# Layer norm normalised by ScalarE, and a rebuilt first batch, in a two-layer ternary feed-forward kernel on one core

## The reference, cut to what matters

```python
h = relu(einsum(x, w1[lang]) + b1[lang])            # 256 -> 64
v = x + einsum(h, w2[lang]) + b2[lang]              # 64 -> 256
normed = (v - mean(v)) * rsqrt(var(v) + 1e-5)
z = normed * gamma[lang] + beta[lang]
def bitlinear(x, W, b):
    w_scale = clip(mean(abs(W)), EPS)
    Wq = clip(round(W / w_scale), -1, 1) * w_scale
    x_scale = clip(max(abs(x), axis=-1), EPS)       # per token
    xq = clip(round(x * 127 / x_scale), -128, 127) * x_scale / 127
    return xq @ Wq.T + b
x = x + bitlinear(gelu(bitlinear(z, W1, b1)), W2, b2)   # 256 -> 1024 -> 256
```

## Time and profile before

| what | value |
|---|---|
| median of 3 runs | 342.05 us |
| the three runs | 339.6, 342.05, 342.3 us |
| the profiled execution | 338.81 us, of which the span from first to last instruction is 336.9 us |
| mean granted TensorE clock | 0.939 |
| layer 0 up to the first instruction of layer 1's dequantisation | 168.0 us |
| layer 1 from there | 168.9 us |

### The profile page before, as it was taken

The page is one execution under the profiler, slowest core; times in us unless marked ns, Lnnn a source line. Parts: engine busy times, 40 slices in busy tenths (PEclk is TensorE's granted clock), DMA queues, the critical chain, the costliest instruction groups (busy, mean ns, idle before and its releaser), DMA issues.

```text
span 336.9 us, 6456 instructions
## 1 busy us (share of the span) xinstructions
PE 270.9 (80%) x1640; PEld 177.6 (53%) x1640; DVE 287.9 (85%) x633; ACT 221.2 (66%) x341; POOL 264.8 (79%) x440
## 2 busy tenths in 40 slices
PE   0783849998799988899777799798989989766775
PEld 0322324563446455466544578576666757535652
DVE  0199599999999989887399899999999999999661
ACT  0641787776667777773256797877778687877560
POOL 2068898888988878862899999898989999899520
PEclk9955898999999999999799989999999999999786
DMA  7987306587879897477681044669677575554863
GB/s 223 298 220 270 110 2 154 135 219 186 192 184 198 184 258 168 115 149 163 175 255 58 2 82 123 173 156 178 142 166 183 102 177 142 90 142 109 180 149 94
DMA packets 97002, 53.10 MB, mean 158 GB/s; under 512 B 74165, under 2 KB 90301, under 8 KB 96966
## 3 DMA queue, kind: packets, MB, share of 16 engines
q1 hardware_dynamic: 95078, 51.43, 62.4%
q10 hardware_dynamic: 1888, 1.27, 1.3%
HBM read 27.51 MB, written 8.39 MB: 107 GB/s over the span
## 4 chain that ended last, share of the span: by engine, by line
issue 28%; POOL 20%; PE 17%; DVE 17%; DMA 8%; ACT 5%; SPq 4%; DVEq 1%; POOLq 0%; ACTq 0%
POOL mid L713 8%; DMA q1T<-r 6%; PE banks L1146 4%; POOL raw_all L720 3%; PE banks L1132 3%; PE banks L1091 3%; POOL xb L693 3%; PE banks L1263 2%; DVE amy L919 2%; DVE xb L913 2%; PE banks L1133 2%; DVE xb L937 2%; POOL dq L704 1%; DVE zg L849 1%; DVE am L950 1%
## 5 line engine op out<-in xcount | busy, mean ns | idle before, releaser
L720 POOL TENSOR_TENSOR raw_all<-raw_all,mid 128x1024 f32<-128x1024 f32 x32 | 64.0, 2014 | 0.2 <-DVE raw_all L944 0.2
L564 ACT ACTIVATE banks<-xb,taps 128x512 f32<-128x512 f32 x64 | 43.6, 689 | 22.5 <-DVE xb L937 22.5
L713 POOL TENSOR_SCALAR mid<-xb,taps,convb 128x512 f32<-128x512 f32 x64 | 49.7, 786 | 2.1 <-DVE xb L937 2.1
L944 DVE SCALAR_TENSOR_TENSOR raw_all<-xb,taps,banks 128x512 f32<-128x512 f32 x64 | 45.6, 735 | 0.0
L937 DVE TENSOR_TENSOR xb<-banks,dqb 128x512 f32<-128x512 f32 x64 | 42.6, 680 | 1.0 <-PE banks L1237 1.0
L1263 PE MATMUL banks<-tern,q1T 128*128 128x256 bf16 x256 | 36.2, 289 | 8.5 <-DVE o L971 5.3
L880 DVE TENSOR_REDUCE am<-g 128x1 f32<-128x1024 f32 x32 | 38.6, 1205 | 3.7 <-ACT g L510 3.7
L1237 PE MATMUL banks<-yT,tern 128*128 128x512 bf16 x128 | 35.0, 383 | 7.4 <-ACT yT L550 3.9
L1146 PE MATMUL banks<-tern,q1T 128*128 128x256 bf16 x256 | 34.1, 277 | 8.4 <-DMA q1T<-r 6.3
L950 DVE TENSOR_REDUCE am<-g 128x1 f32<-128x1024 f32 x32 | 38.7, 1208 | 1.7 <-ACT g L570 1.7
L666 POOL TENSOR_SCALAR r<-g,qs 128x1024 uint16<-128x1024 f32 x24 | 30.8, 1281 | 11.7 <-DVE qs L892 11.7
(11 more groups left out here) (108 smaller groups left out, 561.2 us busy)
## 6 DMA issues: line engine op xcount, KB each, us to landing
xr<-in_x SPq DMA_DIRECT2D x8, 512.0 KB, 4.2
x_after_layer<-x SPq DMA_DIRECT2D x16, 256.0 KB, 2.5
x<-x_after_layer SPq DMA_DIRECT2D x8, 512.0 KB, 3.6
xr<-x_after_layer SPq DMA_DIRECT2D x8, 512.0 KB, 3.8
out_y<-o SPq DMA_DIRECT2D x32, 128.0 KB, 2.0
xT<-in_xT SPq DMA_DIRECT2D x4, 512.0 KB, 4.1
x2T<-in_xT SPq DMA_DIRECT2D x4, 512.0 KB, 5.4
wl<-in_cwl SPq DMA_DIRECT2D x8, 256.0 KB, 3.3
```

The costliest lines, as they stand in the source:

```text
L564: act.activation(bank(BANK_U[g % 3]), apad[:, f, 2:S + 2], ACT.Copy, scale=taps[:, f, 2:3]).then_inc(p_last, 1)
L713: pool.tensor_scalar(mid[f // 2 % 2][:, f % 2, :], apad[:, f, 1:S + 1], taps[:, f, 1:2], convb[:, f:f + 1], ALU.mult, ALU.add).then_inc(p_ ...
L720: pool.tensor_tensor(c[:, 2 * q:2 * q + 2, :], c[:, 2 * q:2 * q + 2, :], mid[q % 2][:, :, :], ALU.add).then_inc(p_sum, 1)
L944: dve.scalar_tensor_tensor(out=conv[b % 2][:, f, :], in0=apad[:, f, 0:S], scalar=taps[:, f, 0:1], in1=bank(BANK_U[(KH * b + f) % 3]), op0= ...
```

## The change

Three things change together.

**Layer norm.** DVE `centre` and `normalise` (eight instructions of 128x256 per batch) go. POOL gets `negative_ratio` (-mean * rstd, 128x2). ACT gets `normalise`, two activations of 128x256 per pair with scale rstd and bias nratio per row, into the single buffer `zg`. DVE gets `gain` (zg * gamma) and `shift` (+ beta), one instruction of 128x512 each per pair. `negative_mean` moves from POOL to DVE. `round1` of tile 2 moves from ACT to POOL, which then rounds all four.

**Ternary weights 1 to 3.** DVE keeps `ternary(0)`. For 1 to 3 ACT `scaled_weights` divides by the scale and rounds in place, POOL `clipped_weights` clips, and ACT `ternary` writes the result.

**The start.** SP waits for the first ids only and issues the loads of batch 0 ahead of the slots; the weights 2 are loaded before the weights 1. ACT runs one small gelu first, so that its table is loaded once, and sums weights 0 before the first relu. PE runs 14 products on ones before its first real one. All `slot1` orders are written anew.

```diff
@@ SP: before the slots
+            sp.dma_start(xT[0][:, :, :], xT_tiles[0]).then_inc(s_ldT[0], 16)
+            sp.wait_ge(s_ids, 16)
+            load_adapter_weights(0)
+            load_tokens(0)
+            load_second(0)
+            load_norm(0)
+            sp.dma_start(ids_sb[:, B:2 * B], t["ids1"]).then_inc(s_ids, 16)
             run(slot1, seam, slot2)
...
@@ ACT
+            act.wait_ge(s_ones, 1)
+            act.activation(tiny[:, :], ones[:, 0:1], ACT.Gelu)
+            def scaled_weights(n):
+                act.wait_ge(s_wsc, 2 * n + 2)
+                act.activation(raw[n], raw[n], ACT.Copy, scale=iws[:, n:n + 1], bias=INTEGER).then_inc(s_wround, 1)
+            def ternary(n):
+                act.wait_ge(s_wclip, n)
+                act.activation(tern[n][:, :], raw[n], ACT.Copy, bias=-INTEGER).then_inc(s_tern[n], 1)
...
+            def normalise(b, p):
+                act.wait_ge(s_nratio, pair(b, p))
+                wait(act, s_z, pair(b, p - 1))
+                for k in range(2):
+                    ins = act.activation(zg[:, k, :], xx[p][:, k, :], ACT.Identity, scale=rstd[p][:, k:k + 1],
+                                         bias=nratio[p][:, k:k + 1])
+                ins.then_inc(s_norm, 1)
...
+            weight_sum(0)
+            identities()
...
@@ POOL
+            def clipped_weights(n):
+                pool.wait_ge(s_wround, n)
+                pool.tensor_scalar(raw[n], raw[n], INTEGER + 1.0, INTEGER - 1.0, ALU.min, ALU.max).then_inc(s_wclip, 1)
...
+            def negative_ratio(b, p):
+                pool.wait_ge(s_rstd, pair(b, p))
+                pool.wait_ge(s_nmean[p], b + 1)
+                wait(pool, s_norm, pair(b - 1, p))
+                pool.tensor_tensor(nratio[p][:, :], nmean[p][:, :], rstd[p][:, :], ALU.mult).then_inc(s_nratio, 1)
...
@@ DVE
-            def centre(b, p):
-                dve.wait_ge(s_nmean, pair(b, p))
...
-                for k in range(2):
-                    ins = dve.scalar_tensor_tensor(out=zg[:, k, :], in0=xx[p][:, k, :], scalar=nmean[p][:, k:k + 1],
-                                                   in1=gam[b % 2][:, :], op0=ALU.add, op1=ALU.mult)
-                ins.then_inc(s_zg, 1)
-
-            def normalise(b, p):
+                dve.tensor_tensor(zg[:, :, :], zg[:, :, :], gam[b % 2][:, :].unsqueeze(1).to_broadcast([P, 2, D]),
+                                  ALU.mult).then_inc(s_zg, 1)
+
+            def shift(b, p):
                 dve.wait_ge(s_zg, pair(b, p))
-                dve.wait_ge(s_rstd, pair(b, p))
                 wait(dve, s_rz, pair(b - 1, p))
...
+                dve.tensor_tensor(z[p][:, :, :], zg[:, :, :], bet[b % 2][:, :].unsqueeze(1).to_broadcast([P, 2, D]),
+                                  ALU.add).then_inc(s_z, 1)
...
@@ PE
+            for _ in range(14):
+                pe.matmul(bank(BANK_UP + 3)[:, 0:P], ones[:, :], ones[:, :], start=True, stop=True)
```

More of the change, by code:

```diff
@@ L21 @@
 QMAX = 127.0
+INTEGER = float(3 << 22)
 CODE = 128.0
@@ L114, in build_program @@
         squares_out = [o2[k // 2][:, :].bitcast(BF16)[:, (k % 2) * D:(k % 2 + 1) * D] for k in range(4)]
+        nratio = [sb(f"nratio{k}", [P, 2]) for k in range(2)]
         vare = [sb(f"vare{k}", [P, 2]) for k in range(2)]
@@ L281, in on, with later @@
                 op(b, *k)
+        def later(op, b):
+            if b > 0:
+                on(op, b)
         def once(s, at, op, *k):
@@ L480, in squares @@
             def squares(b, p):
-                act.wait_ge(s_nmean, pair(b, p))
+                act.wait_ge(s_nmean[p], b + 1)
                 wait(act, s_rstd, pair(b - 1, p))
@@ L517, in round1 @@
                                bias=CODE).then_inc(s_r1[j], 1)
+            weight_sum(0)
+            identities()
             def slot1(s):
+                once(s, B + 2, lead, 0, 1)
+                on(normalise, s - 1, 0)
                 on(adapter_hidden, s)
[L521 to L522 removed]
+                on(round_z, s - 2, 1)
                 on(gelu, s - 3, 3)
[L524 removed]
                 on(squares, s - 1, 1)
[L526 to L528 removed]
+                once(s, 1, scaled_weights, 1)
+                once(s, B + 2, lead_scales, 0)
+                once(s, 3, scaled_weights, 2)
                 on(gelu, s - 2, 0)
                 once(s, 0, weight_sum, 1)
[L531 removed]
                 on(untranspose_z, s - 2, 1)
+                on(normalise, s - 1, 1)
                 on(round_z, s - 1, 0)
[L534 to L535 removed]
+                once(s, 4, scaled_weights, 3)
                 on(gelu, s - 2, 1)
                 on(squares, s, 0)
+                once(s, 2, weight_sum, 3)
+                once(s, 3, ternary, 2)
+                on(gelu, s - 2, 2)
+                once(s, 1, ternary, 1)
                 on(untranspose_z, s - 1, 0)
[L539 removed]
+                once(s, B + 1, lead, 0, 0)
+                once(s, 4, ternary, 3)
+                once(s, 0, weight_sum, 2)
             def lead(b, k):
@@ L835, in add_adapted @@
                 dve.wait_ge(s_ldx[b % 2], 16 * (b // 2 + 1))
-                wait(dve, s_zg, pair(b - 1, p))
-                wait(dve, s_ssq, pair(b - 1, p))
+                wait(dve, s_norm, pair(b - 1, p))
                 for k in range(2):
@@ L975, in slot1 @@
             def slot1(s):
+                once(s, 0, weight_scale, 0)
+                once(s, 0, bias_parts)
+                on(inverse1, s - 3, 3)
+                once(s, 3, weight_scale, 3)
+                once(s, B + 2, absmax_y, 0)
                 on(add_adapted, s, 0)
+                on(scale_z, s - 1, 0)
+                on(inverse_z, s - 1, 0)
+                on(absmax1, s - 2, 0)
+                on(gain, s - 1, 1)
                 once(s, B + 2, scale_y, 0)
-                on(scale_z, s - 1, 0)
@@ L988, in slot1 @@
-                on(normalise, s - 1, 1)
-                on(inverse1, s - 2, 0)
-                once(s, 1, ternary, 1)
+                on(shift, s - 1, 1)
+                on(add_adapted, s, 1)
                 on(absmax1, s - 2, 1)
+                on(scale1, s - 2, 1)
+                on(inverse1, s - 2, 1)
+                on(final1, s - 3, 2)
                 on(absmax_z, s - 1, 1)
-                on(scale1, s - 2, 1)
-                once(s, 3, weight_scale, 3)
-                on(add_adapted, s, 1)
@@ L996, in slot1 @@
-                on(final1, s - 3, 2)
-                on(inverse1, s - 2, 1)
                 on(scale_z, s - 1, 1)
-                on(centre, s, 0)
+                on(inverse_z, s - 1, 1)
                 on(absmax1, s - 2, 2)
-                on(inverse_z, s - 1, 1)
+                on(final1, s - 3, 3)
                 on(scale1, s - 2, 2)
-                once(s, 4, ternary, 3)
-                once(s, 0, ternary, 0)
-                on(final1, s - 3, 3)
+                on(gain, s, 0)
+                on(inverse1, s - 2, 2)
@@ L1006, in slot1 @@
+                on(negative_mean, s, 1)
                 once(s, B + 1, linear, 0, 0)
-                on(normalise, s, 0)
+                on(shift, s, 0)
                 once(s, 0, weight_scale, 1)
-                on(inverse1, s - 2, 2)
+                on(absmax_z, s, 0)
+                on(absmax1, s - 2, 3)
+                on(scale1, s - 2, 3)
                 once(s, 1, weight_scale, 2)
-                on(absmax1, s - 2, 3)
-                on(absmax_z, s, 0)
-                on(scale1, s - 2, 3)
```

150 lines of the change are left out of this document (73 added, 77 removed).

## The result

The changed kernel took 347.87 us (median of 4 runs, 346.1 to 348.5) against 342.18 before; the ratio is 1.0174, 95% interval 1.0122 to 1.0226. It is slower, where 336.0 and a range up to 342.5 had been forecast. The profiled execution took 347.63 us with a span of 345.9.

A forecast was written before the change was run, and what follows sets the result against it. DVE was taken to set the pace of middle batches, PE 0.3 us below, and latency the start. Start −4.2, weights 2 and 3 −1.0 and middle −1.0 summed to −6.2 us: 342.05 to 336.0, range 331 to 342.5.

The forecast's parts named there:

- The start: Up to the first gelu: −4.2 us (from −8 to +1), the first gelu at 38.5 in place of 42.7.
- with 6.3 us to landing they are there at about 18: Start: weights 1, issued near 12 us, land at about 18, so the first squares start near 20.
- The warmed product: Start: 14 products on ones may warm PE for the first adapter product of 3.63 us, saving 1.8 us or nothing.
- The earlier id load: Start: first id load issued one instruction earlier, so the first adapter product comes forward from 9.25 us by some 0.4.
- Weights 2 and 3: Periods from batch 0 to 3: moving their ternary work to ACT and POOL gives −1.0 us (from −3 to +2).
- Each matrix then costs about 1.6 instead of 3.1: Ternary 2 and 3: ACT and POOL each lose up to 1.6 us per matrix, where 3.1 us were lost before.
- The middle batches: Undisturbed batches: −0.2 us each, five times, −1.0 us (from −3.5 to +6), with PE setting the pace.
- as the period stood 0.4 above its busiest engine before, I take 14.1: Middle batches: period of 14.1 us where it was 14.30, with PE busiest at 13.6 and POOL at 13.5.
- The tail: Last gelu to layer 1, and layer 1 itself: 0 us (from −1 to +1), the chain unchanged.
- The port rival: Middle batches: wide DVE operations and POOL wait for each other, POOL 15.3 or period 15.7; 346.5 us, chance 0.11.
- The start gives nothing: Rival: ACT waits longer for weights 1; start 0, weights 0, middle −1, giving 341 us; chance 0.22.
- same: Whole kernel: a time within 1% (3.4 us) of the old one, given chance 0.21, beside faster 0.68 and slower 0.11.

The follow-up runs named there:

- e6: Changed kernel with weights 1 loaded ahead of weights 2, and the sum of weights 2 moved to slot 1 behind the squares: 341.20 us, ratio 0.9976.
- e16: e6 with the ternary forms of weights 1, 2 and 3 back on DVE at their old places: 344.11 us, ratio 1.0108.
- e15: e6 without the 14 products on ones ahead of PE's work: 344.08 us, ratio 1.0027.
- e5: Kernel before with only the layer norm changed (normalise on ACT, ratio on POOL, gain and shift on DVE): 344.44 us, ratio 1.0109.
- e10: e6 with PE's up projection of tile 3 ahead of the adapter's product for the next batch again: 343.00 us, ratio 1.0029.
- e12: e6 with the old layer norm back on DVE: 338.95 us, ratio 0.9831, the ratio from two runs.
- e17: e12 with POOL's split of the first pair's scales ahead of the rounding of tile 3: 340.91 us, ratio 0.9962.
- e8: Kernel before with the rebuilt start alone, weights 1 and their order as before: 342.58 us, ratio 1.0016.
- e9: Changed kernel with the old layer norm back on DVE at the places of gain and shift: 342.86 us, ratio 1.0040.
- e13: e6 with the old norm on DVE, tile 2 rounded on ACT and tile 3's up projection ahead of the adapter's product: 343.16 us, ratio 1.0020.
- e14: e6 with POOL's split of the first pair's scales ahead of the rounding of tile 3: 342.02 us, ratio 1.0031.
- e3: Kernel before with only PE's up projection of tile 3 moved behind the next adapter product: 344.60 us, ratio 1.0046.
- e19: Changed kernel with half of POOL's residual addition left out (output wrong, only its time is of use): 343.93 us, ratio 1.0072.
- e1: Changed kernel with PE's up projection of tile 3 ahead of the adapter product again: 345.71 us, ratio 1.0068.
- e2: Changed kernel with SP issuing the next batch's adapter loads one slot earlier, behind the transpose of tile 0: 349.15 us, ratio 1.0142.
- e4: Kernel before with the next batch's adapter loads issued a slot earlier, behind the transpose of tile 0: 347.27 us, ratio 1.0125.
- e11: e6 with the rounding of tile 2 put back on ACT: 348.19 us, ratio 1.0182.
- e18: e14 with half of POOL's residual addition left out (output wrong, only its time is of use): 343.45 us, ratio 1.0003.

## Why the prediction was wrong

- **The start, −4.2 forecast, −0.9 measured.** The step that failed is "with 6.3 us to landing they are there at about 18". The load took 8.4 us beside the others (issued first it took 7.4 in e6 and 6.2 in e16, so the order is only part of it); the squares came 2.4 us later than the 20 forecast, another 0.4 was lost up to the inverse scale and 0.7 up to the transposes (34.92, forecast about 31.3), and the first gelu came at 41.83, forecast 38.5. That the wait for this load held the chain back is shown by e6: with the load first it has its transposes at 31.49 and its first gelu at 38.65. That this is the forecast 38.5 is luck, since e6's squares came 1.9 ahead of the forecast and no sum stood behind them; the lead went where the prediction hadn't looked. One 128x2 operation of POOL (L683) took 1.89 us beside DVE's ternary 0, where 0.19 is usual, and the sum of weights 2 now stood ahead of ternary 1. Nor did the gain come from taking ternary 1 off DVE, as the prediction had it: with that back on DVE (e16) the first gelu is 2.1 earlier still. The clip took 1.89 (2.4 taken, and 2.0 given as the least). The warmed product saved 1.7 us in the changed kernel, ahead of the 8.6 us in which ACT waited for weights 1 in any case; in e6 it was not warm (3.67), and e15, without the 14 products, is not later. The earlier id load gave nothing: the first cb was issued at 3.50 instead of 5.63, and the product began at 9.25 both times.
- **Weights 2 and 3, −1.0 forecast.** The three periods from batch 0 to 3 take 49.8 us in the changed kernel and 49.9 in e6, against 48.4, so +1.4 and +1.5. The direction is right against the old form in the same order (e16: 55.6). In e6 the period 1 to 2 rose by 1.7, where 1.2 was forecast, but 0 to 1 and 2 to 3 gained nothing (+0.2 and −0.5) where 2.2 in sum was forecast. The term that was mis-sized is "Each matrix then costs about 1.6 instead of 3.1".
- **The middle batches, −1.0 forecast, about +6.5 measured (all of +8.0 but the weights' part).** The loads were right within 0.5 us for every engine. The step that failed is "as the period stood 0.4 above its busiest engine before, I take 14.1". In before's order the new norm does reach 14.12 in one period (e5), without the fourth rounding on POOL; in the change's order an undisturbed period is 15.1 (e6), and the changed kernel hardly has one. Queues that are in order on five engines wait for each other round a ring, through small loads, SP's transposes and POOL's split, and the slack of 0.4 wasn't a constant. Which of these links sets the 15.1 stays open.
- **The tail, 0 forecast:** −1.4. Layer 1: no change that can be told from its scatter.
- **The rivals.** The port rival gave 346.5, near the result, but not by its sum: POOL is busy 13.7 and not 15.3, and gamma and beta take 0.70 and 0.68 in a middle period. The rule of the Trainium skill (SBUF — State Buffer, "SBUF: two separate sides": of a VectorE operation with two SBUF inputs and a GpSimd operation, the one that starts first holds the shared port pair for the whole instruction) agrees with the row of 1.51 us beside the clip. In a middle period of the changed kernel gamma and beta lost next to nothing, but two small operations of POOL beside them took 0.64 and 0.76 instead of 0.2, 1.0 us in all; the rival's price was 1.8, and before the change POOL had such time too, in its roundings (1.38 on the mean then, 1.23 now). "The start gives nothing" was nearest on the start. (Its chance of 0.22 can't fit under the 0.21 given to "same"; the chances don't add up by a hundredth or more.) No rival had what happened: waits between engines that grow although no engine is busy for more than 14.1 of a period of 15.75.

Shown: the order of two weight loads, with the sum that goes with it, carries 6.7 us, start and middle; four different edits (weights first, old norm, tile 3 ahead, half the residual) gain 1 to 2% each on the changed kernel; the first and third don't add up (e10), and whether the first two do stays open (e12 says yes on two runs, e17 no). Argued only: that part of what they gain is periods in which PE no longer waits and its clock doesn't fall. The stretches at 1.2 GHz in the middle of layer 0, with the medians: none in e12 (338.9); one in before, e5, e8, e9, e13, e14 and e17 (340.9 to 344.4); two in e3, e6, e10 and e19 (341.2 to 344.6); three in the changed kernel, e1, e2, e4, e11, e16 and e18 (343.4 to 349.2); four in e15 (344.1). By the times of the profiled executions themselves it is 341.8 for none, 338.8 to 345.1 for one, 341.1 to 347.6 for two, 343.0 to 349.7 for three and 345.2 for four. That is a loose trend, from one profile each, and it doesn't say which is cause.

## What to carry to other kernels

Summing engine loads tells when a kernel can't be faster, not how fast it is: once no engine fills its period, look for the ring of waits, and give each load's landing time a range (a 1 MB load took from 4.8 to 8.4 us in these two kernels). An operation that stands ahead of a long-latency wait in an in-order queue is the first thing to look at; swapping two loads here gave 6.7 us, where taking 13.8 us of work off VectorE gave none. Try a change in parts: the norm alone cost 1.1% and the start alone gave nothing that the runs can show, and the kernel with the lowest median, 338.95 us, is the change without its norm and with weights 1 first.
